# Sorted edge records placed edge by edge instead of in runs padded to eight, in a one-core graph layer

## What is computed

```python
# N, D, E = 6250, 256, 100000
xn = _layernorm(x)
messages = xn[dst] * edge_weight[:, None]
agg = segment_sum(messages, src, num_segments=N)
x = x + (relu((xn + agg) @ W1 + b1) @ W2 + b2) + mix(xn)
x = x + ffn(_layernorm(x))       # top-2 of 16 experts, then a layernorm
```

## Time and profile before

| | us |
|---|---|
| runs, median of three (range) | 2090.82 (2090.57 to 2094.75) |
| the profiled execution, its own time | 2086.33 |
| its span in the trace | 2084.2 |
| counting, up to the last copy of counts | 0 to 54 |
| tables on DVE | 54 to 94 |
| positions on DVE | 94 to 162 |
| sorting by matrices and scatters | 162 to 412 |
| reading back | 412 to 426 |
| gathers | 426 to 1514 |
| rest of the slots, lists | 1514 to 1560 |
| experts and output | 1560 to 2084 |

### The profile page before, as it was taken

The page is one execution under the profiler, slowest core; times in us unless marked ns, Lnnn a source line. Parts: engine busy times, 40 slices in busy tenths (PEclk is TensorE's granted clock), DMA queues, the critical chain, the costliest instruction groups (busy, mean ns, idle before and its releaser), DMA issues. The chain is left out here.

```text
span 2084.2 us, 43884 instructions
## 1 busy us (share of the span) xinstructions
PE 1814.0 (87%) x12300; PEld 1634.0 (78%) x12300; DVE 1411.1 (68%) x4015; ACT 741.2 (36%) x2167; POOL 1206.1 (58%) x1244
## 2 busy tenths in 40 slices
PE   6306999758889999999999999999977999999986
PEld 4206889657878888888888888878766999999974
DVE  5899788758996777677767776657554555555547
ACT  5806778500101333333333332222222333333347
POOL 1003444477777777777777777777703555555424
PEclk9657999979999999999999999999978999999999
DMA  5000101054444444444444444444425642222248
GB/s 174 0 0 21 39 22 39 22 166 149 137 132 120 129 127 129 130 134 129 128 129 128 130 125 125 123 121 128 120 84 163 208 126 72 72 72 72 69 148 316
DMA packets 130018, 232.33 MB, mean 111 GB/s; under 512 B 25990, under 2 KB 82616, under 8 KB 129703
## 3 DMA queue, kind: packets, MB, share of 16 engines
q0 software_dynamic: 56096, 144.39, 23.8%
q1 hardware_dynamic: 46039, 59.76, 8.8%
q10 hardware_dynamic: 27696, 25.83, 3.9%
HBM read 187.46 MB, written 42.43 MB: 110 GB/s over the span
## 5 line engine op out<-in xcount | busy, mean ns | idle before, releaser
L1337 POOL DMA_INDIRECT lower<-xn_rows,lower x858 | 826.9, 964 | 261.5 <-issue 232.8
L1502 DVE TENSOR_SCALAR lower<-bank,lower 128x128 f32<-128x128 f32 x960 | 347.1, 404 | 69.6 <-issue 53.1
L1362 PE MATMUL bank<-ones,ident 128*128 128x128 f32 x2376 | 322.5, 278 | 23.3 <-DVE xh L1519 17.8
L1362 PEld LDWEIGHTS bank<-ones,ident 128*128 128x128 f32 x2376 | 307.4, 192 | 40.4 <-DVE xh L1519 20.7
L1378 PE MATMUL bank<-lower 128*128 x960 | 292.2, 386 | 19.9 <-SPq L1207 13.1
L1519 DVE TENSOR_TENSOR xh<-xh,bank 128x256 f32 x480 | 199.3, 415 | 158.4 <-PE bank L1379 156.9
L1379 PE MATMUL bank<-lower 128*128 x960 | 287.3, 380 | 0.0
L608 POOL DMA_INDIRECT edge_records_sorted<-lower x112 | 113.2, 1011 | 292.3 <-ACT lower L771 266.7
L2003 DVE TENSOR_SCALAR arena<-bank,b_tile 128x128 f32<-128x128 f32 x456 | 128.4, 345 | 166.4 <-PE bank L1881 166.4
L1881 PEld LDWEIGHTS bank<-arena 128*128 128x128 f32 x1824 | 224.6, 194 | 14.6 <-ACT arena L1936 8.9
L1881 PE MATMUL bank<-arena 128*128 128x128 f32 x1824 | 225.6, 278 | 8.1 <-ACT arena L1936 8.1
(11 more groups left out here) (347 smaller groups left out, 2594.7 us busy)
## 6 DMA issues: line engine op xcount, KB each, us to landing
lower<-xn_rows,lower POOLq DMA_INDIRECT x858
lower<-in_L_ffn_w SPq DMA_DIRECT2D x16, 512.0 KB
upper<-in_L_ffn_w SPq DMA_DIRECT2D x16, 512.0 KB
xn_rows<-xh SPq DMA_DIRECT2D x7, 896.0 KB, 4.1
lower<-xn_rows ACTq DMA_DIRECT2D x49, 128.0 KB
xn_rows<-lower ACTq DMA_DIRECT2D x49, 128.0 KB
x_plus_beta<-lower ACTq DMA_DIRECT2D x49, 128.0 KB
upper<-in_x SPq DMA_DIRECT2D x1, 6144.0 KB
```

The costliest lines, as they stand in the source:

```text
L1337: pool.indirect_dma_start(edge_rows[:, t % ROUND, :], None, xn_dram, bass.IndirectOffsetOnAxis(source.bitcast(U32)[:, t:t + 1], 0)).then_i ...
L1362: pe.matmul(sums_at(u)[:, 0:P], ident[:], ones[:], start=True, stop=True)
L1502: dve.tensor_scalar(edge_sel[:, (2 * u + h) % ESEL, :], iota_gather, lane[:, at:at + 1], weight_s[:, at:at + 1], ALU.is_equal, ALU.mult).t ...
```

## The change

Three things change together.

1. **Positions.** A run no longer begins at a multiple of eight for each (bucket, group). Within a bucket the runs of the groups follow one another edge by edge, and only a bucket is rounded up (with 14 places to spare). The addresses of a scatter count edges (8 bytes), not quads (64 bytes); each index still writes 64 bytes, and the end of a run's last quad overlaps the next group's run. So the scatters of a group wait until all of the group before have landed. `ET` becomes 790 (from 858), `UT` 444 (from 480), the table of zeros 792 columns of edges (from 864).
2. **Tables.** The counts come after d = 2, 4, ..., 14. Their totals go by a small DMA to 49 partitions, one per bucket, and the tables are small operations on 49 partitions; PE does the transposes and sums, between the last steps d. `start` and `pos` are 16-bit, in the order of columns that `bkt_c` has, and `bkt_f` goes. The matrix of address steps is bfloat16 and has its steps in three pieces (114 rows for 50); PE multiplies it with two columns of steps in place of one of ones.
3. **Sorting loop.** PE transposes the sum of a group behind the matmuls of the next group, with two buffers `quads_across`; ACT copies accordingly. Of the order of buckets three operations over 2401 elements go (L980 to L987).

```diff
-    ET = -(-(NGRP * ((GC * P + NT * (QE - 1)) // QE)) // (2 * TQ)) * 2
+    QUADS = (P * EC + NT * 2 * (QE - 1)) // QE
+    ET = -(-QUADS // (2 * TQ)) * 2
...
+    rec_from_edge = rec_dram.rearrange("t (e w) -> (t e) w", w=REC)
...
-        start = carve(NBG)
+        start = carve(NBG // 2).bitcast(U16)
...
-        pos = carve(EC)
+        pos = carve(EC // 2).bitcast(U16)
...
+            sp.wait_ge(s_cnt, NR)
+            sp.dma_start(totals[0:NT, :], cnt[0:1, :]).then_inc(s_early, 16)
             with sp.Fori(0, NG) as g:
...
             def scatter(r, i):
                 g = r * GPR + i
                 pool.wait_ge(s_qcp, g + 1)
+                pool.sem_inc(s_apart, 1)
                 pool.wait_ge(s_qidx, g + 1)
                 pool.sem_inc(s_apart, 1)
+                if i:
+                    pool.wait_ge(s_scat[i - 1], (r + 1) * (16 * NQ))
+                    pool.sem_inc(s_apart, 1)
+                elif looped(r) or r >= 1:
+                    pool.wait_ge(s_scat[GPR - 1], r * (16 * NQ))
+                    pool.sem_inc(s_apart, 1)
                 for c in range(NQ):
-                    pool.indirect_dma_start(rec_dram, bass.IndirectOffsetOnAxis(quad_idx[i][:, c:c + 1], 0),
+                    pool.indirect_dma_start(rec_from_edge, bass.IndirectOffsetOnAxis(quad_idx[i][:, c:c + 1], 0),
                                             quads[i][:, c * QW:(c + 1) * QW], None).then_inc(s_scat[i], 16)
...
-                if d % 4 == 3:
-                    count(d // 4)
...
+                if d % 2 == 0 and d <= 2 * NR:
+                    count(d // 2 - 1)
+                sums(d)
...
                 mm.then_inc(s_qmm, 1)
+                if i:
+                    turn(r, i - 1)
+                elif looped(r) or r >= 1:
+                    turn(r - 1, GPR - 1)
...
-            dve.wait_ge(s_pref, 2 * len(BANKS))
...
+            dve.wait_ge(s_early, 32)
+            dve.tensor_scalar(totals_i[kb, :], totals[kb, :], float(QE - 1), None, ALU.add).then_inc(s_dve, 1)
+            dve.tensor_tensor_scan(upto_g[kb, :], ones[kb, 0:NGRP], totals[kb, :], 0.0, ALU.mult, ALU.add).then_inc(s_dve, 1)
...
-                    dve.copy_predicated(bg2(pos), bg2(masks[(b - 1) % 4]), start[:, (b - 1) * NGRP:b * NGRP].unsqueeze(2)
-                                        .to_broadcast([P, NGRP, GC])).then_inc(s_dve, 1)
+                    dve.copy_predicated(columns(pos), columns(masks[(b - 1) % 4]), start[:, (b - 1) * NGRP:b * NGRP].unsqueeze(1)
+                                        .to_broadcast([P, GC, NGRP])).then_inc(s_dve, 1)
```

More of the change, by code:

```diff
@@ L322, in gps_layer @@
         kvs = carve(DC * P)
-        base, bucket_key, bucket_rank, bucket_of = (kvt[:, k * NT:(k + 1) * NT] for k in range(4))
+        base, bucket_of = (kvt[:, k * NT:(k + 1) * NT] for k in range(2))
         kvm_flat = kvm.rearrange("p c e -> p (c e)")
@@ L613, in edges_gpsimd @@
                       channel_multiplier=FAR * P, allow_small_or_imprecise_dtypes=True).then_inc(s_zero, 1)
-            pool.wait_ge(s_recz, 16)
-            with pool.Fori(0, NG) as r:
+            pool.wait_ge(s_early, 32)
+            for i in range(GPR):
+                scatter(0, i)
+            with pool.Fori(1, NG) as r:
                 for i in range(GPR):
@@ L789, in edges_scalar @@
                 rounds(r)
+            copy_across(NG - 1, GPR - 1)
+            copy_quads(NG - 1, GPR - 2)
             copy_quads(NG - 1, GPR - 1)
@@ L835, in edges_vector @@
+            dve.wait_ge(s_dve, n.add())
+            then(dve.tensor_tensor(upto_g[kb, :], upto_g[kb, :], bucket_fq8[kb, :], ALU.subtract))
+            dve.wait_ge(s_pref, 2)
+            dve.tensor_scalar(ahead[kb, :], keys_at[kb, :], key_col[kb, :], None, ALU.is_gt).then_inc(s_small, 1)
             for c, (b0, nb) in enumerate(BANKS):
-                dve.tensor_scalar(quads_i[:, b0 * NGRP:(b0 + nb) * NGRP], bank[c][:, 0:nb * NGRP], float(QE - 1), None,
-                                  ALU.add).then_inc(s_dve, 1)
+                at = slice(b0 * NGRP, (b0 + nb) * NGRP)
+                dve.wait_ge(s_pref, 3 + c)
+                dve.scalar_tensor_tensor(start[:, at], cnt[:, at], not_first, bank[2 * c][:, 0:nb * NGRP], ALU.mult, ALU.add).then_inc(s_dve, 1)
```

275 lines of the change are left out of this document (141 added, 134 removed).

## The result

| | before | after |
|---|---|---|
| runs, median of four (range), us | 2090.70 (2086.75 to 2094.75) | 1953.08 (1941.20 to 1957.18) |
| ratio, 95% interval | | 0.933 (0.929 to 0.938) |
| the profiled execution, us | 2086.33 | 1952.81 |
| its span | 2084.2 | 1951.0 |
| first masked copy | 94.25 | 56.51 |

The change takes 137.6 us off the median. The range was 1914 to 1955, so the time lies in it, close to its upper end, and 24 us above the 1929 that I named. Of the 133.5 us between the two profiled executions, 38.0 had been gained when the first matrices began, 14.4 more by the first gather, 85.0 over the gathers, and 4.2 were lost behind the start of the last one (the rest is the difference between span and execution).

The account below looks back on a forecast made before the run. No engine bounds throughout; POOL bounds the gathers, an engine-to-engine chain the sorting loop. Gathers 86.3, tables 49.3 and loop 29.0, less 3.0, save 161.6 us: 2086.3 to 1924.7, named as 1929 for the runs' median; range 1914 to 1955.

Parts of the forecast that it names:

- the rival of 1938 to 1940: Gather stage: PE or DVE takes POOL's place as the bound, so the whole takes 1938 to 1940 us; chance 0.10.
- stalls in the heads: Gather stage: POOL stalls in heads, which come every 9 units, not every 9.7; 1.5 us lost (0 to 6).
- the double rate: Tables: the 16-bit masked copy runs twice as fast, ACT then bounds, first matrices at 112.5, 49.3 us earlier.
- The other end of the bounds: Tables: masked copy stays at the old rate, first matrices at 124.7, 37 us earlier, whole 1942 us; chance 0.27.
- my 7.0 us: Sorting loop: POOL's new chain per group, three scatter pitches of 1.27 us plus 3.2 us from last scatter to landing.
- the 7.15: Sorting loop: predicted period per group in us, where it was 8.37; stage 29 us shorter, bounds 17 to 36.
- The rival that overlapping, unaligned writes land later: Sorting loop: landings of 3 us cost 20 us, whole 1949; chance 0.08 for landings of 2.8 to 3.5 us.
- 6.33, 0.24 and 0.6: Sorting loop, PE's step per group: matmuls, 0.24 for the transpose, some 0.6 for eight bfloat16 rows, given as 6.95 us.
- a landing of 9.5 us: Sorting loop, slower-than-before rival: landings that long put the whole at 2127 us; chance of slower 0.01.
- The fuller tail: End of the gather stage: slots stay dense to the end, 1.5 us lost.
- my two rivals: Masked copy no faster in 16 bits, 1942 us (0.27); overlapping, unaligned writes landing at 3 us, 1949 us (0.08).

Follow-up runs that it names:

- pe_pos: Changed kernel with the masked copy replaced by DVE products that PE adds to the ranks: median 2229.84 us, 13.4 less than the changed kernel there.
- psum_codes: Changed kernel with one operand of DVE's codes product (L994) read from PSUM, not SBUF; only the sorting loop counts: 197.9 us, where it had 207.2.
- aligned: Changed kernel with each run's first address rounded down to 64 bytes, writes still overlapping; only the sorting stage counts: loop 196.0 us against 217.0.
- stripes: Changed kernel with groups sorted in turn from two stripes, each following the landing of the group before the previous: median 2225.59 us, 17.6 less.

## Why the prediction was right, and what was off

*Gathers.* Right: 68 columns less, 85.0 us for the 86.3 predicted, as a column took 1.270 us and not 1.2685. Neither PE nor DVE took POOL's place: the rival of 1938 to 1940 did not happen there. PE waited 3.5 us for landings behind 660 us, not more than before. The 1.5 us that I put on stalls in the heads did not show.

*Tables.* The sum was right to half a microsecond, its terms were not: they cancelled, which is luck. The last copy of counts came at 42.50 (43.4 predicted), the small DMA had DVE start again at 45.22, 2.4 us behind the copy's end (3.0 assumed), and from there to the first mask, at 55.84 (55.3 predicted), it was 10.6 us where I had 8.5. In 3.9 of them DVE waits for PE's sums.

*Masked copy.* **Wrong**, and the step that I had called the least certain of my choices. I took the double rate, because all operands now had one type and layout; the instruction has one rate. 0.97 us instead of 0.62, first matrices at 123.84 instead of 112.5. The other end of the bounds was right: 124.7. The row of before, 1.02 us, was a measured price for this very instruction, and I set a rule made for others above it; the Trainium skill's tier table (VectorE: DVE Perf Modes, "The perf-mode tier table") does not name the masked copy, which I had noted and not heeded. That ACT would bound at the double rate was right: I had its root at 109.7, pe_pos has it end at 110.42.

*Sorting loop.* Direction right, the size **half**: 14.2 us gained from the first matrices to the end of the last scatter, where I had 29.0. POOL's chain of pitches and landing became the path, as the part said it might, and its floor was even shorter than my 7.0 us (6.69). The step that failed is the 7.15: I let every landing take 2.1 us and added 0.15 us a group for the rest. Measured were 0.56 us a group for late landings (15.2 / 27) and 0.40 for scatters that DVE held up (10.9 / 27), 7.67 in all, 14.1 us over 27 groups. The rival that overlapping, unaligned writes land later, which got 0.08, was true in kind. Its price was not as it stands: it has 20 us for a landing of 3 us in every group, but the median of 2.9 is one of all scatters, about half of the groups waited no longer than for a quick landing (13 of 27 up to 2.0 us), and psum_codes puts late landings without held scatters at some 2 us above aligned.

The second term, DVE's product in POOL's way, was in no step. The trace of before had three scatters of 1.76 to 3.17 us at its start, which I passed over. Two of them follow the same rule, beside products of two operands in SBUF: 0.97 + 2.33 - 0.12 = 3.18 and 0.97 + 0.92 - 0.12 = 1.77, within 0.01 us of the rows.

```profile
189.56 2.65 DVE L980 TENSOR_TENSOR xh<-iota_n,arena 128x2401 f32<-128x2401 f32 x1
189.88 3.17 POOL L608 DMA_INDIRECT edge_records_sorted<-lower  x1 [0.31 <-issue]
192.25 2.66 DVE L983 TENSOR_TENSOR xh<-xh,arena 128x2401 f32<-128x2401 f32 x1
193.99 1.76 POOL L608 DMA_INDIRECT edge_records_sorted<-lower  x1 [0.94 <-ACT lower L771]
```

Nor would quick landings have given the 7.15: with them the loop went at 7.26 (aligned) and 7.25 (stripes), and the rows of stripes show PE waiting for ACT's weights, a path that the part did not price. Two sums of the prediction do not add up as they stand: 6.33, 0.24 and 0.6 make 7.17 and not 6.95 (PE's step was 6.75, since these overlap), and a landing of 9.5 us would give 2125 and not 2127. Neither moved the forecast.

*Tail.* The fuller tail cost 4.2 us behind the last gather where I had put 1.5. Between the last unit and the first expert matmul lie 53.0 us (1384.7 to 1437.7), where there were 47.1 (1523.0 to 1570.1). What in the slots makes them was not tried.

*The sum.* 1924.7 predicted, 11.3 for the masked copy, 14.8 for the sorting stage, 2.7 for the tail, 1.3 for the gathers less the 1.5 of stalls that did not come, and 0.5 less in small differences: 1952.8, which the execution took. The range held by 2 us, and in part by luck. Alone my two rivals would have ended at 1942 and 1949; they came together, a case for which the list has no chance, and had the late landings cost the 20 us of their rival, the time would have lain outside.

## What to carry to other kernels

An order that costs nothing in one schedule (1.0008 in the kernel before) becomes the path once the schedule around it is faster; price it by the landing that the new writes will have, against what the rest of the loop can do, and let it reach one step further back where the data allow: two stripes took 17.6 us off. When an instruction has a row, its row is its price until a run shows another. An engine that no longer waits drifts through the others' work, and then meets holds that its old place had hidden.

## What the runs showed of the hardware

- Writes of 64 bytes to DRAM that begin at any multiple of 8 bytes and overlap bytes of an earlier group land late (median 2.9 us, up to 5.1, where 2.1 is the quickest). With one of the two properties alone POOL waited 4 and 7 times in 27 groups and the loop took 196.0 and 198.3 us. With both it waited 26 times and the loop took 217.0, of which 9 to 10 us are held scatters and not landings. The mechanism is open.
- A product of two operands in SBUF on DVE (128x896, 1.08 us) holds up a scatter that POOL starts beside it, by what is left of it, less 0.12 us. With one operand in PSUM none of the 14 that began beside it was held for that rest.
- The masked copy of 784 elements takes 0.97 us with 16-bit operands, flat or broadcast, and 1.02 with 4-byte data; a bitwise operation on the same 16-bit operands takes 0.56, the comparison that makes the mask 0.41.
- One program took 1953 us in one place and 2243 in another, and the kernel before 2087 to 2091 and 2382 to 2385: most of it in the gather stage (1.27 and 1.60 us a column), for a reason that was not found. The change gained about the same in both, 138 and 142 us, though in the second POOL was held for places for some 300 us.
